# Two spectral layers on one core: image reloads, sums and differences at other places in the order, forward stores of twice the size, and a first image through all PSUM banks

## The reference

```python
f = jnp.fft.fft2(xf, axes=(1, 2), norm='ortho')
Xk = (f.real - f.imag)[:, lo:hi, :kept]           # 45 x 23 frequencies kept
o1 = relu(einsum('bhwni,nio->bhwno', Xk, w1[0]) + b1[0])
o2 = einsum('bhwni,nio->bhwno', o1, w2[0]) + b2[0]
y = jnp.fft.ifft2(spec_with(_softshrink(o2, LAM)), s=(H, W), ...).real
return y + x
```

## Time and profile before

| | |
|---|---|
| median of 3 runs | 598.96 us (593.26 to 599.08) |
| the profiled execution | 594.54 us, of which span 592.6 us |
| mean granted clock of TensorE | 0.947 |
| busy: TensorE / VectorE / POOL / ACT | 479.6 / 361.8 / 276.7 / 211.1 us |
| DMA | 108.29 MB, mean 183 GB/s |

### The profile page before, as it was taken

One profiled execution on the slowest core, in us unless ns is written; L12 is line 12 of the kernel. 1 busy time (PEld: TensorE's weight loads), 2 busy tenths in 40 slices (PEclk: granted clock), 3 DMA queues, 4 the chain that ended last, 5 costly groups with the idle time before them and its releaser, 6 DMA issues.

```text
span 592.6 us, 16944 instructions
## 1 busy us (share of the span) xinstructions
PE 479.6 (81%) x6944; PEld 334.2 (56%) x6944; DVE 361.8 (61%) x728; ACT 211.1 (36%) x485; POOL 276.7 (47%) x267
## 2 busy tenths in 40 slices
PE   1418789998898899798888899699997899997763
PEld 0015568776575667476566566566675666775411
DVE  6625456686576667475747656656776767666532
ACT  1203344544234433253234333254334433443101
POOL 9916542661456424671357523674258522322123
PEclk9999789999998999898997989989999999999958
DMA  8659966364897959794796938968698967633587
GB/s 179 209 115 156 210 150 169 100 176 119 226 239 150 236 144 245 210 219 136 205 256 146 243 100 207 255 151 223 168 236 206 222 188 186 165 106 100 129 222 207
DMA packets 81617, 108.29 MB, mean 183 GB/s; under 512 B 10441, under 2 KB 67903, under 8 KB 81414
## 3 DMA queue, kind: packets, MB, share of 16 engines
q1 hardware_dynamic: 64044, 61.01, 37.7%
q0 software_dynamic: 11024, 40.46, 30.0%
q10 hardware_dynamic: 6474, 5.76, 5.0%
HBM read 53.97 MB, written 53.19 MB: 181 GB/s over the span
## 4 chain that ended last, share of the span: by engine, by line
PE 41%; DMA 24%; DVE 14%; POOL 10%; issue 5%; ACT 2%; SPq 2%; POOLq 0%; DVEq 0%; ACTq 0%
DMA img<-x 20%; PE ps L718 8%; PE ps L667 6%; PE ps L705 6%; PE ps L743 6%; PE ps L624 5%; PE ps L654 5%; DVE img L595 4%; DVE uv L517 4%; POOL y L419 3%; POOL xs L397 3%; DVE ns L571 3%; SPq L327 2%; DMA jr<-scr_i 2%; ACT p L486 2%
## 5 line engine op out<-in xcount | busy, mean ns | idle before, releaser
L411 POOL TENSOR_TENSOR uv<-img 128x768 f32<-128x768 f32 (+1 forms) x48 | 101.6, 2128 | 29.9 <-DMA img<-x 29.5
L419 POOL DMA_DIRECT2D y<-img x56 | 40.1, 718 | 138.7 <-DVE img L595 134.5
L654 PE MATMUL ps<-jr,cst 64*64 64x384 f32 (+1 forms) x736 | 83.7, 518 | 13.8 <-DVE img L595 8.0
L718 PE MATMUL ps<-wt,o 128*64 128x96 f32 x1472 | 78.7, 258 | 19.7 <-DVE o L563 19.3
L667 PEld LDWEIGHTS ps<-cst,bt 128*64 128x64 f32 x1472 | 65.6, 148 | 39.1 <-issue 26.2
L718 PEld LDWEIGHTS ps<-wt,o 128*64 128x64 f32 x1472 | 69.3, 143 | 32.4 <-issue 32.4
L517 DVE TENSOR_TENSOR uv<-img 128x768 f32<-128x768 f32 (+1 forms) x48 | 63.2, 1316 | 37.7 <-DMA img<-x 35.2
L667 PE MATMUL ps<-cst,bt 128*64 128x90 f32 x1472 | 74.5, 259 | 13.8 <-DMA bt<-scr_f 13.8
L595 DVE TENSOR_TENSOR img<-ps,img 109x768 f32<-109x768 f32 x76 | 72.5, 955 | 20.9 <-PE ps L654 20.2
L397 POOL TENSOR_TENSOR xs<-xs,nt 128x360 f32<-128x360 f32 (+1 forms) x48 | 41.6, 867 | 87.3 <-DVE nt L549 66.1
L705 PE MATMUL ps<-xs,wt 64*97 64x180 f32 (+1 forms) x768 | 70.5, 321 | 12.0 <-POOL xs L397 11.7
(11 more groups left out here) (44 smaller groups left out, 456.2 us busy)
## 6 DMA issues: line engine op xcount, KB each, us to landing
y<-img POOLq DMA_DIRECT2D x28, 540.0 KB, 8.0
scr_f<-fs SPq DMA_DIRECT2D x384, 36.0 KB
scr_i<-et SPq DMA_DIRECT2D x48, 288.0 KB, 5.1
jr<-scr_i SPq DMA_DIRECT2D x92, 144.0 KB, 5.7
img<-x POOLq DMA_DIRECT2D x24, 540.0 KB, 9.9
bt<-scr_f SPq DMA_DIRECT2D x40, 288.0 KB, 6.6
y<-img POOLq DMA_DIRECT2D x14, 270.0 KB, 6.8
img<-x POOLq DMA_DIRECT2D x12, 270.0 KB, 5.4
```

The lines of the kernel that those rows point to most:

```text
L411: nc.gpsimd.tensor_tensor(uv[n % 2][:, 1, 0:j1 - j0, :], img[t % IMGS][:, j0:j1, 0, :], img[t % IMGS][:, j0:j1, 1, :], ALU.subtract).then_ ...
L654: last = mm(ps[64 * p:64 * p + 64, B0 + a, 0:m], w_inv[c, r, :], set_rows(t, g)[c, p, 0:m], start=True, stop=True)
L718: last = mm(ps[64 * r:64 * r + 64, P2 + p, b * 2 * BS:(b + 1) * 2 * BS], o11[:, b, 2 * p + r, :], w21[:, block_no(s // STEPS, b), :], star ...
```

## The change

Four things change. First, each forward group is stored with four transfers of 72 KB and not eight of 36 KB, both banks in one. Second, the first task's forward products go to banks 2(g mod 4) and the next, so to all eight in turn, and ACT evicts one bank of a group and VectorE the other; the later tasks are as before. Third, the inverse halves are split in the list: `inv` (product) and `add` (VectorE's addition, POOL's store); for the third place of a step the addition moves behind d0. Fourth, the order of a step is now: load; c1; the first group's `uv` (w); first inverse half and addition (w); e; refill of chunk 2 in i = 1; an inverse half and addition (w); c0; the second group's `uv` (w); refill of chunk 0 in i = 5 or 1 in i = 0; d1; an inverse half (w); d0; its addition (w); first `fwd` (w); a; rows in i = 1; refill of chunk 3 in i = 1; second `fwd` (w); t; the last inverse half and addition (w).

```diff
+    def both(group):
+        return [group, ("add",) + group[1:]] if group else []
+
@@ schedule, a step
-        first, last = inv[s][0:len(inv[s]) - 3] if len(inv[s]) > 3 else [], inv[s][max(len(inv[s]) - 3, 0):]
+        groups = [None] * (4 - max(len(inv[s]), 3)) + inv[s]
+        groups += [None] * (4 - len(groups))
         uv = [("uv",) + f[1:] for f in fwd[s]]
-        ahead = [("uv",) + f[1:] for f in fwd[s + 1]] if s + 1 < NSTEPS else []
         if s + 2 < NSTEPS:
             order.append(("load", s + 2))
         if 0 < s <= NSTEPS:
             order.append(("c1", s - 1))
-        order += first
+        order += uv[0:1]
+        order += both(groups[0])
         if s > 1:
             order.append(("e", s - 2))
-        order += uv[1:2]
-        order += last[0:1]
+        if i == 1 and t > 1:
+            order.append(("refill", t - 2, 2))
+        order += both(groups[1])
         if s < NSTEPS:
             order.append(("c0", s))
-        if 0 < s <= NSTEPS:
-            order.append(("d1", s - 1))
-        order += last[1:2]
-        if s < NSTEPS:
-            order.append(("d0", s))
+        order += uv[1:2]
         if i == 5 and t > 0:
             order.append(("refill", t - 1, 0))
         if i == 0 and t > 1:
             order.append(("refill", t - 2, 1))
+        if 0 < s <= NSTEPS:
+            order.append(("d1", s - 1))
+        order += both(groups[2])[0:1]
+        if s < NSTEPS:
+            order.append(("d0", s))
+        order += both(groups[2])[1:2]
...
         if i == 1 and t > 1:
-            order.append(("refill", t - 2, 2))
+            order.append(("refill", t - 2, 3))
...
-        order += last[2:3]
-        order += ahead[0:1]
-        if i == 1 and t > 1:
-            order.append(("refill", t - 2, 3))
+        order += both(groups[3])
@@ SP, fwd
-                    for p in range(2):
-                        sp.wait_ge(f_cp, 2 * n + p + 1)
-                        for a in range(2):
-                            for o in range(2):
-                                sp.dma_start(scr_f[t][o * KWP // 2:(o + 1) * KWP // 2, :, p, g, a].rearrange("k e s c -> (k e) (s c)"),
-                                             fs[k][64 * a + 32 * o:64 * a + 32 * o + KWP, p, :]).then_inc(f_st[k], 16)
+                    sp.wait_ge(*(f_cp, 2 * (n - CH + 1)) if t else (f_act, n + 1))
+                    if t == 0:
+                        sp.wait_ge(f_dve, n + 1)
+                    for a in range(2):
+                        for o in range(2):
+                            sp.dma_start(scr_f[t][o * KWP // 2:(o + 1) * KWP // 2, :, :, g, a].rearrange("k e p s c -> (k e) p (s c)"),
+                                         fs[k][64 * a + 32 * o:64 * a + 32 * o + KWP]).then_inc(f_st[k], 16)
@@ POOL, the store of a chunk
-                if kind == "inv" and what[0] < TASKS - 1 and (what[1] + 1) // 2 in [b for a, b in CHUNKS] and what[1] % 2 == 1:
+                if kind == "add" and what[0] < TASKS - 1 and (what[1] + 1) // 2 in [b for a, b in CHUNKS] and what[1] % 2 == 1:
@@ ACT, fwd
-                    for p in range(2):
-                        nc.scalar.activation(fs[n % FS][:, p, :], ps[:, P3 + p, 0:2 * HC], ACT.Copy).then_inc(f_cp, 1)
+                    if t == 0:
+                        nc.scalar.activation(fs[n % FS][:, 0, :], ps[:, 2 * (g % 4), 0:2 * HC], ACT.Copy).then_inc(f_act, 1)
+                    else:
+                        for p in range(2):
+                            nc.scalar.activation(fs[n % FS][:, p, :], ps[:, P3 + p, 0:2 * HC], ACT.Copy).then_inc(f_cp, 1)
@@ DVE
+                if kind == "fwd" and what[0] == 0:
+                    g = what[1]
+                    if g >= FS:
+                        dve.wait_ge(f_st[g % FS], 64 * (g // FS))
+                    dve.wait_ge(f_mm, g + 1)
+                    nc.vector.tensor_copy(fs[g % FS][:, 1, :], ps[:, 2 * (g % 4) + 1, 0:2 * HC]).then_inc(f_dve, 1)
...
-                if kind == "inv" and (what[0] < TASKS - 1 or what[1] not in LAST_POOL):
+                if kind == "add" and (what[0] < TASKS - 1 or what[1] not in LAST_POOL):
@@ PE, fwd
-                    vacate(0)
-                    vacate(1)
+                    B0 = P3 if t else 2 * (g % 4)
+                    if t > 0:
+                        vacate(0)
+                        vacate(1)
+                    elif g >= 4:
+                        pe.wait_ge(f_act, g - 3)
+                        pe.wait_ge(f_dve, g - 3)
```

More of the change, by code:

```diff
@@ L178, in schedule @@
             order.append(("t", s - 1))
-        order += last[2:3]
-        order += ahead[0:1]
-        if i == 1 and t > 1:
-            order.append(("refill", t - 2, 3))
-    order += held
+        order += both(groups[3])
+    order += [e for h in held for e in both(h)]
     order += [("rows", TASKS - 1, j) for j in range(CH)]
-    order += [("inv", TASKS - 1, g) for g in range(GROUPS)]
+    order += [e for g in range(GROUPS) for e in both(("inv", TASKS - 1, g))]
     return order
@@ L243, in spectral_layers @@
         f_mm, f_cp = sem("fwd_product"), sem("fwd_copied")
+        f_act, f_dve = sem("first_fwd_copied_act"), sem("first_fwd_copied_dve")
         f_st = [sem(f"f{k}_stored") for k in range(FS)]
@@ L333, in _ @@
                         for n in range((t + 1) * CH - FS, (t + 1) * CH):
-                            sp.wait_ge(f_st[n % FS], 128 * (n // FS + 1))
+                            sp.wait_ge(f_st[n % FS], 64 * (n // FS + 1))
                     if s < BT:
@@ L364, in _ @@
                                      scr_i[t][:, :, a, 4 * j:4 * j + 4, :].rearrange("k e h c -> (k e) (h c)")).then_inc(landed, 16)
-                if kind == "inv" and what[0] == TASKS - 1 and what[1] % 2 == 1:
+                if kind == "add" and what[0] == TASKS - 1 and what[1] % 2 == 1:
                     g, (b, f) = what[1] // 2, divmod(TASKS - 1, HALVES)
@@ L426, in _ @@
                         pool.dma_start(folded(k, p, j0, j1), rows_of(x[b], HR * p + j0, HR * p + j1, f)).then_inc(x_ld[k][c], 16)
-                if kind == "inv" and what[0] == TASKS - 1 and what[1] in LAST_POOL:
+                if kind == "add" and what[0] == TASKS - 1 and what[1] in LAST_POOL:
                     t, (g, r) = what[0], divmod(what[1], 2)
@@ L448, in _ @@
                     if n >= FS:
-                        act.wait_ge(f_st[n % FS], 128 * (n // FS))
+                        act.wait_ge(f_st[n % FS], 64 * (n // FS))
                     act.wait_ge(f_mm, n + 1)
-                    for p in range(2):
-                        nc.scalar.activation(fs[n % FS][:, p, :], ps[:, P3 + p, 0:2 * HC], ACT.Copy).then_inc(f_cp, 1)
+                    if t == 0:
[3 more added lines that the diff above has]
+                            nc.scalar.activation(fs[n % FS][:, p, :], ps[:, P3 + p, 0:2 * HC], ACT.Copy).then_inc(f_cp, 1)
                 if kind == "x":
@@ L623, in _ @@
                                 q, m = 64 * p, 64 * a + 32 * o
-                                last = mm(ps[m:m + 32, P3 + p, 0:2 * HC], w_fwd[q:q + 64, o, :],
+                                last = mm(ps[m:m + 32, B0 + p, 0:2 * HC], w_fwd[q:q + 64, o, :],
                                           uv[n % 2][q:q + 64, o, 2 * a:2 * a + 2, :].rearrange("w s c -> w (s c)"), start=True, stop=True)
@@ L627, in _ @@
                     for p in range(2):
-                        tenant[p] = [(f_cp, 2 * n + p + 1)]
+                        tenant[p] = [(f_cp, 2 * (n - CH) + p + 1)] if t else []
                 if kind == "inv":
@@ L658, in _ @@
                     s, = what
+                    if s == 0:
+                        pe.wait_ge(f_act, CH)
+                        pe.wait_ge(f_dve, CH)
                     if s >= 3:
```

## The result

| | before | changed |
|---|---|---|
| median | 596.11 us | 623.36 us (621.61 to 629.37) |
| ratio | 1 | 1.0478 (95% interval 1.0371 to 1.0584) |
| span of the profiled execution | 592.6 us | 619.8 us |

The change made the kernel 4.8% slower. The forecast was 588 us, the range 568 to 610; rival A, the slower one, had been given 603 to 608, and 618 in its worst case.

A forecast was written before the change was run, and what follows sets the result against it. TensorE, busy 81% of the span, was held to lose mostly idle time and slow clock, chiefly from `uv` waiting for image reloads. Start -11, rounds +3.8, last steps -0.5 made -7.7 from 594.54: 587, put at 588 us, range 568 to 610.

The forecast's parts named there:

- rival A: Slower: store 1 queues fully behind reload 0, X = 17.3; round 71.3 us, time 603 to 608, worst 618; chance 0.28.
- The new waits in steps 5 and 0: POOL waits for image stores before d0's subtraction; step 5 from 11.5 to 13.4 us, step 0 from 9.1 to 14.2.
- X: Step 0: time from reload 0's issue to store 1's landing; taken as 14 us, between 10.5 and 17.6.
- POOL's waiting: POOL's wait at the reload for the image's store (`y<-img`), forecast to rise from 1 us to 20 to 40 in total.
- What they buy: Earlier reloads: step 1 from 14.5 to 10.8 us, including 1.7 of slow clock; step 3 from 13.0 to 10.6.
- The addition behind d0: Third inverse group's addition and store issue leave the path from d1 to next c1; steps 4 and 5 gain 0.4 us each.
- if step 3 stays at 13: One of three signs that the prediction is wrong; step 3 was forecast to fall from 13.0 to 10.6 us.
- `uv` on both engines at once: Step 2 rises from 8.9 to 9.2 us, as VectorE's `uv` then takes 2.14 us and not 0.96.
- The start: First product of stage a at 32.2 us, 7.9 earlier; with `uv` behind c1 and c0, -11 us (-3 to -13).
- Rival D: Start doesn't gain, as a double-size store takes twice as long to issue: 8 us more per case; chance within the others.
- Nothing from the halved stores in the rounds: Half the store issues on SP are worth nothing in the rounds, as no engine waits there for `bt` or `jr`.
- The sum: Round 68.1 us against 67.35; -11 + 3.8 - 0.5 = -7.7 from 594.54 gives 587, forecast put at 588.

The follow-up runs named there:

- b_refill_early: Kernel before with only the reloads of chunks 0 and 1 moved behind c0, ahead of d1 and d0: 607.71 us, ratio 1.012.
- a_add_i3: Changed kernel with the third inverse place's addition ahead of d0 again, in steps i = 3 alone: 609.89 us, ratio 1.015.
- a_flat: Changed kernel with the forward scratch laid out so a row's two banks lie side by side, still 24 stores in the start: 621.48 us, ratio 1.041.
- a_split: Changed kernel with eight stores of 36 KB a group again: 623.14 us, ratio 1.044.
- a_uv_apart: Changed kernel where, from task 1 on, POOL starts a difference only after VectorE's sum of the same row group: 608.24 us, ratio 1.021.

## Why the prediction was wrong, point by point

**The new waits in steps 5 and 0: right, and nearly of the right size.** 12.9 and 15.2 us against 13.4 and 14.2. The time called X was 315.3 - 300.56 = 14.7 us, against 14 taken. Rival A's 17.3 did not come about; the slower result was not its mechanism. But POOL's waiting, forecast as 20 to 40 us, was 68.5, though the steps that it ends came out nearly as forecast.

**What they buy: right in step 1.** Step 1 took 11.5 (10.8 forecast, 14.5 before), and b_refill_early has it at 11.0. The extra is the clock: in the round shown, the longest of the five, TensorE took 13.10 us for what takes 8.8, behind 4.3 us of waiting. The forecast of 1.7 us for that clock was too small there. What the early reloads were to bring in step 3 did not show, for the reason that follows.

**The addition behind d0: wrong, and the largest miss.** Step 3 took 14.0 and not 10.6, +3.4 a round or 17 us in all. The prediction said that the addition "leaves the path from d1 to the next c1" and asked only who is held up by it on VectorE. It did not ask who waits for the banks that it empties. In step 3 a forward product stands right behind d0 and uses them; the row L644 waiting for L610 shows it, and a_add_i3 took the step back to 11.4. That is 2.6 of the 3.4 us. The other 0.8 was a miss of the sum with the addition in its old place as well: a_add_i3 still has 1.17 to 1.70 us of that wait, and the sum had none. With the addition late the prediction's own sign came true, that it is wrong "if step 3 stays at 13".

**`uv` on both engines at once: right mechanism, wrong size.** Step 2 took 11.5 and not 9.2, +2.3 a round or 11 us. The 2.14 us of the earlier trace rows was taken as the price and the 0.96 of the earlier trace rows as the sum undisturbed, but both had one difference of POOL beside them; in the earlier trace rows it had begun first. With two in a row ahead the sum takes 3.70 us. The refill between the differences of step 2 had kept them apart before. The clock is in the 11.5 too: step 2 took 10.5, 10.6 and 10.9 us in three rounds at 1.00, and 12.4 and 12.9 in two at 0.86 and 0.87. Two of the five, with the columns of the tables by window:

```profile
255.80:266.33 10.53, 8.80 (x149) 6.39 (x148) 8.22 (x13) 5.04 (x13) 6.21 (x6) 1.00 0.75 193
...
405.21:417.63 12.42, 10.36 (x150) 7.55 (x149) 8.55 (x13) 5.21 (x13) 6.72 (x8) 0.86 0.80 204
```

The Trainium skill ("GPSIMD Engine Reference", Key points) says that GpSimd shares its SBUF interfaces with VectorE, with contention where a VectorE instruction has two SBUF inputs. The trace agrees, 3.70 us against 0.94 with nothing beside it. That page gives no size.

**The start: wrong in its main term.** The forecast was 32.2 us for the first product of a and 11 us of lead at step 11; measured were 38.65 and 5.5. Of the 5.5 only the 1.4 us at the first product are clear of the scatter at step 11. The failing term is 0.45 us for a store of twice the size, derived from a load of 288 KB; the other bound, 0.9, was the closer. Rival D said so in words and was priced at 8 us. The measured issue is 0.76. In a_flat, where it is 0.37, the product still comes at 33.96: the evictions had waited up to 4.2 us for stores to free `fs`, and the last ended at 27.1, not 25.4. The sum had nothing for that.

**Nothing from the halved stores in the rounds: right** (the ratio of a_split, 1.044, is within 0.4% of the changed kernel's).

**The sum.** 68.1 was forecast for a round and 74.5 measured: over the steps 5, 0, 1, 2, 3, 4 the misses are -0.5 +1.0 +0.7 +2.3 +3.4 -0.4. Five times 6.4 is 32 us, the start 5.5 more, the end 2.5 less: 35 us, which takes the profiled 587 to 622. The range came mainly from the sizes of the two store waits and of the start. The two terms of the rounds that broke it, step 3's addition and step 2's sum, had been given no bound. Put right alone they gave 13 and 15 us; both together without the late reloads was not run.

**What stays open.** What makes a store in two places a row dear to issue is not known. In step 2 of the changed kernel the granted clock fell behind a wait of 2.06 us in one round, but not behind the same 2.06 us in the round shown; why is open. It was not tried to issue the reloads from a queue where no computation stands behind them.

## What to carry to other kernels

When an eviction or an addition is moved later in an in-order list, look for who waits for the memory that it frees, not only for who waits for its result. Here the wait for a store cost less where its data was used than on a queue with work behind it (21.3 us more of the one against 50.7 less of the other made the kernel 23 us faster): of two places for the same dependency, count what stands behind each. And when a step is moved, look at what it used to keep apart: a reload's issue between two of POOL's differences had left the time for VectorE's sum, and one added wait was worth 15 us.

## What the runs showed of the hardware

The issue of a store on SP followed the form of its pattern and not its bytes: 0.37 us for 24 rows of 1536 or of 3072 bytes, 0.76 us for 24 rows in two pieces of 1536. The count of pieces alone is no rule, as transfers of 384 pieces of 768 bytes took 0.32 and 0.47 us. A pair of stores of 1.1 MB from `img`, issued on POOL, took 10.9 us to land with nothing of its queue ahead (10.1 for the second of them), and 12.5 behind a reload of the same size.

VectorE's sum of two SBUF operands, 0.94 us with nothing beside it, took 2.1 beside one POOL operation of 1.8 us that had begun first and 3.7 beside two, ending 0.8 us after them: it nearly stood still while POOL worked. Where the sum had begun first it took 0.96, and POOL's difference 2.58 and not 1.82. POOL's durations are rough in this profile.

TensorE's waits often cost clock behind them. In the round shown, 4.33 us were followed by a step that was busy for 13.10 us at 0.64 where 8.8 is usual, so they cost as much again; 2.97 us by 10.71 us at 0.86 against 8.66 in the kernel before; and 2.29 us by a clock of 0.88 in step 3. But the length of one wait does not settle it: a_uv_apart has the same 2.29 us in its five steps 3, and the clock was 0.88 in two of them and 1.00 in three.
